# Keys of even and odd columns from one TensorE matmul, and a rotary product that writes to other partitions than it reads

## The chip, the core and the metric

The kernel runs on one core of one Trainium2 chip. The metric is device time in microseconds (us). Three runs of the kernel before gave 519.69, 520.85 and 522.8 us; the median, 520.85 us, is the time before.

## What is computed

Two layers on x of 8 sequences by 256 tokens by 128 columns. Each layer normalises x, and adds an attention and a mixture of experts of the normalised x. The change lies in the second layer's attention, which has 16 query heads and 4 key heads of 8 columns each, with a rotary position code on queries and keys:

```python
def _apply_rotary(x, freqs):
    x1, x2 = (x[..., ::2], x[..., 1::2])
    cos, sin = (jnp.cos(freqs), jnp.sin(freqs))
    return jnp.concatenate([x1 * cos - x2 * sin, x1 * sin - x2 * cos], axis=-1)
...
q = (x @ Wq + bq).reshape(Bx, Tx, NH, HD).transpose(0, 2, 1, 3)
k = (x @ Wk + bk).reshape(Bx, Tx, NKV, HD).transpose(0, 2, 1, 3)
q = _apply_rotary(q, freqs)
k = _apply_rotary(k, freqs)
scores = jnp.einsum('bhqd,bhkd->bhqk', q, k) / jnp.sqrt(jnp.float32(HD))
```

## The kernel before

The work goes by sequence (called a batch in the code, b = 0 to 7) and layer (L = 0, 1). A hand-written plan (`attention_plan`) is a list of items in steps t = 0 to 18. Each engine walks the same list and does its part of each item, in that order, waiting on semaphores. A step has 12 units u. In step t four batches are in flight: `a` is projected (`qk`, `hi`, `lo`, `stack`, `val`), `b` has its natural-order scores and their row maxima taken (`nat`, `max`), `c` its transposed scores and exponentials (`st`, `exp`), `d` its output finished (`pv`, `otr`, `norm`, `ott`, `proj`, `res`). The second layer's batches are projected in steps 8 to 15. Between steps 13 and 14 stands the second layer's mixture of experts (`moe`), with GpSimd's scatters (`scat`, from step 12) before it and its gathers (`back`) behind it.

The order at the head of a second-layer step is what the change touches. All of it is in unit 0, in this order:

- TensorE, `qk`: waits for PSUM banks M1 and M0 and multiplies the transposed x (256 columns) by WqA and WqB, the even and odd columns of Wq, into M1[:, 0:256] and M1[:, 256:512] (L1428), then by WkA and WkB into M0[0:32, 0:256] and M0[0:32, 256:512] (L1431). Then come `nat` and `st` of unit 0, the last `pv` of `d` (L1520), and unit 1.
- VectorE, `rotary` (L1079): waits for M1, writes (even + bias)*cos and (odd + bias)*sin of the queries to slots 0 and 1 of ROT; waits for M0, writes the same of the keys to slots 2 and 3 on partitions 0 to 31 (L1088), and raises `rot_ok`. A row maximum of `b` (L1059) follows.
- GpSimd, `rotate` (L726): waits for `rot_ok`, subtracts slot 1 from slot 0 and slot 3 from slot 2 (L731), raises `rsub_ok`.
- ScalarE, `high` (L802): waits for `rsub_ok`, copies the rounded values to XQ (L814, L815). Only behind that stands the first exponential (L824) of `c`, which frees a bank that `st` of unit 2 needs. There are two such banks, S0 and S1.
- In unit 1, VectorE's `low` (L1063) waits for ScalarE's copy and writes the rounding rest (L1075), ahead of the row maximum of unit 1.

The keys' weights lie side by side in WP[1][:, 512:...] as 32 even and 32 odd columns. The biases lie in a table of constants, one column for even and one for odd, on partitions 0 to 31. The tables cosr and sinr repeat every 8 partitions, so that any block of 32 partitions holds the same values.

Of the kernel before, what the change touches and what calls it, by code (L numbers as in the profile page):

```python
# [11 lines left out]
ALU = mybir.AluOpType  # L12
# [3 lines left out]
P = 128  # L16
NB, T, C = 8, 256, 128
NT = NB * T // P
TPB = T // P
NH, HD = 16, 8  # L20
NKV = 4
# [31 lines left out]
CO_BQ = CO_STEP + E1  # L53
# [8 lines left out]
def constants(w):  # L62

    t = np.zeros((P, NCONST), np.float32)
    r, c = np.arange(P)[:, None], np.arange(P)[None, :]
    t[:, CO_ID:CO_ID + P] = r == c
    t[:, CO_MASK:CO_MASK + P] = np.where(c > r, NEG, 0.0)
    t[:, CO_TRI:CO_TRI + P] = r < c
    t[:, CO_ONE:CO_ONE + P] = 1.0
    inv = (np.float32(1.0) / np.float32(10000.0) ** (np.arange(0, HD, 2, dtype=np.float32) / np.float32(HD))).astype(np.float32)  # L70
    ang = (np.arange(T, dtype=np.float32)[None, :] * inv[:, None]).astype(np.float32)
    cos, sin = np.cos(ang).astype(np.float32), np.sin(ang).astype(np.float32)
    for row in range(P):
        i = row % HD
        a, b = (cos, sin) if i < HD // 2 else (sin, cos)
        t[row, CO_C:CO_C + T] = a[i % (HD // 2)]
        t[row, CO_S:CO_S + T] = b[i % (HD // 2)]
    t[:, CO_I8:CO_I8 + E0] = np.arange(E0)
    t[:, CO_IN:CO_IN + CAP] = np.arange(1, CAP + 1)
    for r in range(4):  # L80
        t[QK_ROWS + 2 * r:QK_ROWS + 2 * r + 2, CO_SEL + r] = 1.0
    t[:, CO_THR:CO_THR + NT] = P * np.arange(NT)
    t[:, CO_PRE:CO_PRE + E1 * E1] = (np.arange(E1)[None, :] < np.arange(E1)[:, None]).reshape(-1)
    t[:, CO_J:CO_J + NTILE] = np.arange(NTILE)
    home = [expert_home(e) for e in range(E1)]
    t[:, CO_STEP:CO_STEP + E1] = np.append(np.diff(home), 0)
    t[:, CO_BQ], t[:, CO_BQ + 1] = w["L0_attn_bq"], w["L0_attn_bk"]
    for a in range(2):
        t[:, CO_BQ + 2 + a] = halves(w["L1_attn_bq"], a)
        t[0:NKV * HD, CO_BQ + 4 + a] = halves(w["L1_attn_bk"], a)  # L90
    t[:, CO_B1:CO_B1 + E0 * HC] = w["L0_ffn_b1"].reshape(E0 * HC, P).T
    t[:, CO_B2:CO_B2 + E0] = w["L0_ffn_b2"].T
    t[:, CO_RW:CO_RW + E1] = w["L1_ffn_router_w"].T
    t[:, CO_LN], t[:, CO_LN + 1] = w["L1_ffn_ln_scale"], w["L1_ffn_ln_bias"]
    for e in range(E1):
        t[:, CO_UB + home[e]:CO_UB + home[e] + HC] = w["L1_ffn_up_b"][e].reshape(HC, P).T
    return t


def halves(x, a):  # L100

    x = x.reshape(x.shape[:-1] + (-1, 1, HD // 2, 2))[..., a]
    return np.concatenate([x, x], axis=-2).reshape(x.shape[:-3] + (-1,))
# [10 lines left out]
def expert_home(e):  # L114

    return (e // 3) * (KS + 16) + KS + 4 + 4 * (e % 3)
# [185 lines left out]
def build(nc, w, table, wp_d, moe_d, out):  # L302
    ctx = ExitStack()
    with ctx:
        def sb(name, shape, dt=F32):
            return ctx.enter_context(nc.sbuf_tensor(name, shape, dt))

        def sem(name):
            return ctx.enter_context(nc.semaphore(name))
# [10 lines left out]
        cosr, sinr = K[:, CO_C:CO_C + T], K[:, CO_S:CO_S + T]  # L320
        identb, maskb, trib, oneb = (sb(n, [P, P], BF16) for n in ("identb", "maskb", "trib", "oneb"))
        WP = [sb(f"WP{L}", [P, x.shape[1]]) for L, x in enumerate(wp_d)]
# [2 lines left out]
        Wo = [WP[0][:, 3 * C:4 * C], WP[1][:, 2 * C + 96:3 * C + 96]]  # L325
        Wr = WP[0][:, 4 * C:4 * C + E0]
        WqAB = WP[1][:, 0:2 * C].rearrange("c (j n) -> c j n", j=2)
        WkAB = WP[1][:, 2 * C:2 * C + 64].rearrange("c (j n) -> c j n", j=2)
        bcol = K[:, CO_BQ:CO_BQ + 6]
        bvb = [sb(f"bvb{L}", [P, C]) for L in range(2)]  # L330
        bob = [sb(f"bob{L}", [P, C]) for L in range(2)]
# [18 lines left out]
        ROT = [sb(f"ROT{i}", [P, 4, T]) for i in range(2)]  # L350
# [56 lines left out]
        bank = {n: ctx.enter_context(nc.psum_tensor(f"ps_{n}", [P, 512], F32)) for n in names}  # L407
# [6 lines left out]
        full = {n: sem(f"full_{n}") for n in names}  # L414
# [106 lines left out]
        def await_free(eng, n, use):  # L521

            if before[n, use] is not None:
                eng.wait_ge(*released(before[n, use]))

        def await_full(eng, n, use):

            eng.wait_ge(*filled[n, use])
# [435 lines left out]
        def _(dve):  # L964
# [9 lines left out]
            for i in range(NV):  # L974
                last = dve.memset(VA[i][:], 0.0)
# [103 lines left out]
            def rotary(b):  # L1079

                i = b % 2
                if b >= 2:
                    dve.wait_ge(qlo_ok, NB + b - 1)
                dve.wait_ge(rc_ok, 1)
                for j, (n, rows, col) in enumerate((("M1", P, 2), ("M0", NKV * HD, 4))):
                    await_full(dve, n, ("qk", 1, b))
                    for a, tab in ((0, cosr), (1, sinr)):
                        last = dve.scalar_tensor_tensor(out=ROT[i][0:rows, 2 * j + a, :],  # L1088
                                                        in0=bank[n][0:rows, a * T:(a + 1) * T],
                                                        scalar=bcol[0:rows, col + a:col + a + 1], in1=tab[0:rows, :],  # L1090
                                                        op0=ALU.add, op1=ALU.mult)
                last.then_inc(rot_ok, 1)

            def values(L, b):
# [238 lines left out]
            def attention(plan):  # L1333
                for at, item in enumerate(plan):
# [5 lines left out]
                    if k == "qk" and item[1] == 1:  # L1340
                        rotary(item[2])
# [40 lines left out]
        def _(pe):  # L1382
            mm = pe.matmul
            M0, M1 = bank["M0"], bank["M1"]
# [31 lines left out]
            def qk(L, b):  # L1416
                x = XT[:, T * b:T * (b + 1)]
                if L == 0:
                    await_free(pe, "M1", ("qk", L, b))
                    for j in range(2):  # L1420
                        last = mm(M1[:, T * j:T * (j + 1)], Wqk0[:, j, :], x, start=True, stop=True)
                    last.then_inc(full["M1"], 1)
                else:
                    await_free(pe, "M1", ("qk", L, b))
                    await_free(pe, "M0", ("qk", L, b))
                    pe.wait_ge(f_in, 16 * 5)
                    for j in range(2):
                        last = mm(M1[:, T * j:T * (j + 1)], WqAB[:, j, :], x, start=True, stop=True)  # L1428
                    last.then_inc(full["M1"], 1)
                    for j in range(2):  # L1430
                        last = mm(M0[0:32, T * j:T * (j + 1)], WkAB[:, j, :], x, start=True, stop=True)  # L1431
                    last.then_inc(full["M0"], 1)

            def val(L, b):
                n = C if L == 0 else NKV * HD
# [264 lines left out]
            def ffn():  # L1700
# [4 lines left out]
                with pe.Fori(0, E0 - 1, 2) as e0:  # L1705
# [14 lines left out]

            layer1 = {"py": slots_out, "po": combine, "px": xt, "pl": logits}
            work = {"qk": qk, "val": val, "nat": nat, "st": st, "pv": pv, "mxt": mxt, "otr": otr, "ott": ott,
                    "proj": proj}

# [51 lines left out]
```

## Time and profile before

| | |
|---|---|
| median of the runs | 520.85 us (519.69 to 522.8) |
| time of the profiled execution | 522.24 us |
| its span in the profile | 520.2 us |
| mean granted TensorE clock in it | 0.96 of full speed |
| busy: TensorE, VectorE, ScalarE, GpSimd | 87%, 62%, 48%, 33% of the span |
| second-layer `qk` of batches 0 to 7 starts at | 212.2, 234.1, 255.3, 276.9, 297.6, 323.4, 438.3, 459.7 us |

The profiled execution is 1.4 us above the median; its span is 2.0 us under its own time. PE is TensorE's matmuls, PEld its weight loads, which run ahead of the matmuls; DVE is VectorE, ACT ScalarE, POOL GpSimd. One fp32 matmul of the program appears as two matmul records. Ends of matmuls are modelled. A granted clock of 1.00 is 2.4 GHz and 0.50 is 1.2 GHz. In brackets behind a row stands how long its engine had been idle before it, and what ended that.

### The profile page before, as it was taken

What the parts mean: (1) busy time and instruction counts of PE and PEld (TensorE: products, weight loads), DVE (VectorE), ACT (ScalarE), POOL (GpSimd) and SP (SyncE); (2) the same over time, 40 slices, a digit from 0 to 9 for tenths busy, and PEclk for the clock granted to TensorE, in tenths of its full rate; (3) what the DMA queues carried; (4) which work ended last, traced back from release to release, by engine and by line L of the source; (5) the groups of instructions that cost most, each with busy time, mean ns of one, the idle gap of its engine ahead of it and who ended that gap; (6) DMA issues with size and microseconds to landing.
All of it is one profiled execution on the core that took longest, in us unless ns stands there. A gap on an engine that the chain in (4) does not pass through costs nothing.

```text
span 520.2 us, 10264 instructions
## 1 busy us (share of the span) xinstructions
PE 452.7 (87%) x3503; PEld 343.1 (66%) x3503; DVE 322.6 (62%) x974; ACT 248.0 (48%) x564; POOL 173.7 (33%) x226
## 2 busy tenths in 40 slices
PE   1668899979999999999988987894999999898985
PEld 1554567758868878677665663663999997554643
DVE  5565741126668868777787795642666665565672
ACT  1731455524655655454464442442565563644452
POOL 6640120003254354444544417771000000737600
PEclk9998999997999999999999997896999999899898
DMA  5553123473223233021162612231221211314220
GB/s 163 134 129 89 63 64 107 122 211 114 68 74 99 69 90 115 15 79 42 42 202 95 192 59 70 87 97 56 62 81 44 81 58 36 102 43 135 52 58 28
DMA packets 51441, 45.89 MB, mean 88 GB/s; under 512 B 4968, under 2 KB 46464, under 8 KB 51392
## 3 DMA queue, kind: packets, MB, share of 16 engines
q1 hardware_dynamic: 47424, 35.54, 23.9%
q0 software_dynamic: 2240, 4.53, 3.2%
q10 hardware_dynamic: 1728, 5.20, 3.0%
q8 instruction: 27, 0.44, 0.3%
q14 instruction: 22, 0.18, 0.1%
HBM read 26.24 MB, written 19.01 MB: 87 GB/s over the span
## 4 chain that ended last, share of the span: by engine, by line
PE 49%; issue 23%; DVE 9%; POOL 8%; DMA 5%; ACT 3%; SPq 1%; ACTq 0%; DVEq 0%; POOLq 0%
PE ps_S L1498 7%; PE ps_P L1520 6%; POOL xs L742 6%; PE ps_N L1469 6%; PE ps_N L1465 4%; PE ps_M L1717 3%; PE ps_M L1563 2%; PE ps_M L1600 2%; PE ps_P L1537 2%; DMA X<-in_L_attn_x 2%; PE ps_P L1554 2%; DVE NM L1059 2%; PE ps_N L1710 2%; PE ps_S L1710 2%; PE ps_M L1574 1%
## 5 line engine op out<-in xcount | busy, mean ns | idle before, releaser
L824 ACT ACTIVATE PT<-ps_S 128x512 f32<-128x512 f32 x192 | 112.6, 592 | 98.5 <-PE ps_S L1498 96.6
L1059 DVE TENSOR_REDUCE NM<-ps_N 128x2 f32<-128x512 f32 (+1 forms) x192 | 128.0, 682 | 46.0 <-PE ps_N L1469 44.8
L1469 PE MATMUL ps_N<-STK 96*128 96x256 f32 (+1 forms) x256 | 103.2, 446 | 0.0
L689 POOL TENSOR_SCALAR_AFFINE_SELECT PT<-PT 128x512 f32<-128x512 f32 x80 | 49.1, 638 | 142.5 <-ACT PT L824 142.5
L1498 PE MATMUL ps_S<-STK 100*128 100x128 f32 (+5 forms) x352 | 92.8, 339 | 3.2 <-ACT PT L824 3.2
L1465 PE MATMUL ps_N<-maskb,identb 128*128 128x256 bf16 (+1 forms) x192 | 62.2, 324 | 6.7 <-DVE NM L1059 6.3
L1498 PEld LDWEIGHTS ps_S<-STK 104*128 104x128 f32 (+1 forms) x352 | 62.3, 199 | 7.5 <-ACT PT L824 4.5
L1520 PE MATMUL ps_P<-PT,VA 128*32 128x256 f32 (+1 forms) x1024 | 56.8, 341 | 0.4 <-ACT PT L824 0.4
L1469 PEld LDWEIGHTS ps_N<-STK 96*128 96x128 f32 x256 | 52.0, 203 | 4.7 <-issue 0.7
L731 POOL TENSOR_TENSOR ROT<-ROT 128x256 f32<-128x256 f32 (+1 forms) x16 | 11.3, 731 | 104.2 <-DVE ROT L1088 104.2
L1520 PEld LDWEIGHTS ps_P<-PT,VA 128*32 128x32 f32 x1024 | 27.2, 111 | 26.8 <-issue 12.6
L916 ACT ACTIVATE LATE<-ps_N,ucol 128x128 f32<-128x128 f32 x104 | 29.6, 369 | 19.3 <-PE ps_N L1666 18.1
L742 POOL DMA_INDIRECT xs<-XN,slot x32 | 31.1, 973 | 19.8 <-DVE slot L1254 10.5
L1465 PEld LDWEIGHTS ps_N<-maskb,identb 128*128 128x128 bf16 x192 | 20.0, 104 | 22.9 <-DVE NM L1059 10.9
L1495 PE MATMUL ps_S<-identb,maskb 128*128 128x256 bf16 (+1 forms) x72 | 24.0, 334 | 7.7 <-ACT PT L824 4.7
L1666 PE MATMUL ps_N<-LATE 128*128 128x128 f32 x208 | 29.6, 288 | 0.5 <-DVE LATE L1280 0.3
L1666 PEld LDWEIGHTS ps_N<-LATE 128*128 128x128 f32 x208 | 26.6, 200 | 1.6 <-issue 0.6
L1283 DVE COPY LATE<-EW 128x512 f32 x39 | 16.6, 427 | 13.7 <-PE ps_P L1676 7.8
L1329 DVE TENSOR_SCALAR LATE<-ps_M,consts 128x320 f32 x8 | 4.4, 551 | 33.2 <-PE ps_M L1717 33.2
L1275 DVE COPY LATE<-EW 128x512 f32 x39 | 16.8, 430 | 10.7 <-issue 5.2
L814 ACT ACTIVATE XQ<-ROT 128x256 fp32r<-128x256 f32 x8 | 3.3, 417 | 39.1 <-POOL ROT L731 39.1
L1676 PE MATMUL ps_P<-LATE 128*128 128x128 f32 x160 | 21.3, 276 | 0.3 <-ACT LATE L916 0.3
(197 smaller groups left out, 818.3 us busy)
## 6 DMA issues: line engine op xcount, KB each, us to landing
STK<-scr SPq DMA_DIRECT2D x96, 96.0 KB
scr<-XQ SPq DMA_DIRECT2D x24, 256.0 KB
ROT<-in_L_ffn_W SPq DMA_DIRECT2D x16, 256.0 KB, 3.1
EW<-in_moe ACTq DMA_DIRECT2D x8, 512.0 KB, 3.4
scr<-XQ SPq DMA_DIRECT2D x24, 128.0 KB
xs<-zero SPq DMA_DIRECT2D x1, 2496.0 KB, 11.1
LATE<-xs SPq DMA_DIRECT2D x9, 256.0 KB, 2.8
ysl<-LATE SPq DMA_DIRECT2D x9, 256.0 KB, 2.3
```

Source lines behind the costliest of these rows:

```text
L689: last = pool.affine_select(out=v, in_=v, compare_op=ALU.is_ge, fill=0.0, base=0, pattern=[[0, 4], [1, P]], channel_multiplier=-1)
L742: pool.indirect_dma_start(xs, bass.IndirectOffsetOnAxis(ap=slot[:, i, k:k + 1], axis=0), XN[:, i, :], None)\
L824: act.activation(PT[:, g, r, :], bank[s][:], ACT.Exp, scale=SCALE).then_inc(exp_ok, 1)
L916: act.activation(E_H[j % 2][:, P * m:P * (m + 1)], bank[UP_BANKS[j % 3]][:, P * m:P * (m + 1)], ACT.Gelu, bias=ucol[j % 2][:, m:m + 1]).th ...
L1059: dve.tensor_reduce(NM[b % 2][:, h, qt, :].rearrange("q (p c) -> q c p", p=2)[:, slots[0]:slots[-1] + 1, :], bank[s][:].rearrange("q (c p ...
L1465: mm(diag, identb[:], maskb[:, None, :].broadcast_to((P, many, P)), start=True, stop=False, skip_group_check=True)
L1469: last = mm(s[:, 2 * w_ * i:2 * w_ * (i + 1)], stk[0:QK_ROWS, c, P * qt:P * (qt + 1)], stk[0:QK_ROWS, k_slots(L, c, 2 * h, 2), 0:w_], star ...
L1495: mm(s[:].rearrange("k (h q) -> k h q", h=len(slots))[:, :, 0:P], maskb[:], identb[:, None, :].broadcast_to((P, len(slots), P)), start=Tru ...
L1498: last = mm(s[:, n * i:n * (i + m)], stk[rows, k_slots(L, c, g, 1), P * kt:P * (kt + 1)], stk[rows, c:c + m, T - n:T], start=not masked, s ...
L1520: last = mm(o, va[:, kt, head, :], pr, start=(kt == 0), stop=(kt == 1))
L1666: last = mm(o[:, P * m:P * (m + 1)], E_W1[j % 2][:, P * m:P * (m + 1)], E_XT[j % 2], start=True, stop=True)
L1676: last = mm(bank[DOWN_BANKS[j % 2]][:, 0:C], E_H[j % 2][:, P * m:P * (m + 1)], E_W2[j % 2][:, P * m:P * (m + 1)], start=(m == 0), stop=(m ...
```

## The change

One matmul per batch, with all 64 columns of the keys' weights, writes the even half to M0[0:32, 0:256] and the odd half to M0[32:64, 0:256]. The odd half's rotary product reads PSUM, bias and table on partitions 32 to 63 and writes ROT on partitions 0 to 31, as before. The bias of the odd half moves to partitions 32 to 63. The counts of semaphores and their places in the order stay as they are.

```diff
@@ constants
-        t[0:NKV * HD, CO_BQ + 4 + a] = halves(w["L1_attn_bk"], a)
+        t[NKV * HD * a:NKV * HD * (a + 1), CO_BQ + 4 + a] = halves(w["L1_attn_bk"], a)
@@ build
-        WkAB = WP[1][:, 2 * C:2 * C + 64].rearrange("c (j n) -> c j n", j=2)
+        WkAB = WP[1][:, 2 * C:2 * C + 64]
@@ rotary
-                for j, (n, rows, col) in enumerate((("M1", P, 2), ("M0", NKV * HD, 4))):
-                    await_full(dve, n, ("qk", 1, b))
-                    for a, tab in ((0, cosr), (1, sinr)):
-                        last = dve.scalar_tensor_tensor(out=ROT[i][0:rows, 2 * j + a, :],
-                                                        in0=bank[n][0:rows, a * T:(a + 1) * T],
-                                                        scalar=bcol[0:rows, col + a:col + a + 1], in1=tab[0:rows, :],
-                                                        op0=ALU.add, op1=ALU.mult)
+                tabs = (cosr, sinr)
+                await_full(dve, "M1", ("qk", 1, b))
+                for a in range(2):
+                    dve.scalar_tensor_tensor(out=ROT[i][:, a, :], in0=bank["M1"][:, a * T:(a + 1) * T], scalar=bcol[:, 2 + a:3 + a],
+                                             in1=tabs[a], op0=ALU.add, op1=ALU.mult)
+                await_full(dve, "M0", ("qk", 1, b))
+                for a in range(2):
+                    r = slice(NKV * HD * a, NKV * HD * (a + 1))
+                    last = dve.scalar_tensor_tensor(out=ROT[i][0:NKV * HD, 2 + a, :], in0=bank["M0"][r, 0:T],
+                                                    scalar=bcol[r, 4 + a:5 + a], in1=tabs[a][r, :], op0=ALU.add, op1=ALU.mult)
@@ qk
-                    for j in range(2):
-                        last = mm(M0[0:32, T * j:T * (j + 1)], WkAB[:, j, :], x, start=True, stop=True)
-                    last.then_inc(full["M0"], 1)
+                    mm(M0[0:64, 0:T], WkAB, x, start=True, stop=True).then_inc(full["M0"], 1)
```

## Rows read from the trace of the kernel before

**Rows 1.** Profile page: span, busy time, and the chain that ended last by engine

```profile
span 520.2 us, 10264 instructions
...
PE 452.7 (87%) x3503; PEld 343.1 (66%) x3503; DVE 322.6 (62%) x974; ACT 248.0 (48%) x564; POOL 173.7 (33%) x226
...
PE 49%; issue 23%; DVE 9%; POOL 8%; DMA 5%; ACT 3%; SPq 1%; ACTq 0%; DVEq 0%; POOLq 0%
```

**Rows 2.** Groups by line and shape: busy us, mean ns of one, idle before

```profile
L1431 PE MATMUL ps_M<-XT,WP 128*32 128x256 f32 x32 | 8.4, 385 | 0.0
L1088 DVE SCALAR_TENSOR_TENSOR ROT<-ps_M,consts 32x256 f32<-32x256 f32 x16 | 6.9, 467 | 0.1
```

**Rows 3.** Chain that ended last: start us, us, what; batches 0, 4 and 6

```profile
213.30 0.98 PE ps_M L1431 x4
...
217.10 0.40 ACT XQ L815
...
299.34 0.58 DVE ROT L1088 x2
...
453.46 0.68 PE ps_P L1554 x4
```

**Rows 4.** Waits over the whole span: us in total, times, longest

```profile
ACT XQ L814 <- POOL ROT L731: 39.1, 8, 5.6
```

**Rows 5.** Timeline of batch 0's projection: start us, us, engine, line

```profile
213.23 1.05 PE L1431 MATMUL ps_M<-XT,WP 128*32 128x256 f32 x4
213.41 1.77 DVE L1088 SCALAR_TENSOR_TENSOR ROT<-ps_M,consts 128x256 f32<-128x256 f32 x4 [0.18 <-PE ps_M L1428]
...
215.11 0.67 DVE L1059 TENSOR_REDUCE NM<-ps_N 128x4 f32<-128x512 f32 x1
215.26 1.42 POOL L731 TENSOR_TENSOR ROT<-ROT 128x256 f32<-128x256 f32 x2 [1.88 <-DVE ROT L1088]
...
216.77 0.42 ACT L814 ACTIVATE XQ<-ROT 128x256 fp32r<-128x256 f32 x1 [4.69 <-POOL ROT L731]
...
217.53 0.75 DVE L1075 TENSOR_TENSOR XQ<-ROT,XQ 128x256 fp32r<-128x256 f32 x2 [1.75 <-ACT XQ L815]
...
218.03 0.66 PE L1498 MATMUL ps_S<-STK 100*128 100x128 f32 x4 [0.80 <-ACT PT L824]
```

**Rows 6.** Timeline of VectorE in batch 1: the four rotary products one by one

```profile
235.37 0.48 DVE L1088 SCALAR_TENSOR_TENSOR ROT<-ps_M,consts 128x256 f32<-128x256 f32 x1 [0.45 <-PE ps_M L1428]
...
235.77 0.48 DVE L1088 SCALAR_TENSOR_TENSOR ROT<-ps_M,consts 128x256 f32<-128x256 f32 x1
...
236.28 0.47 DVE L1088 SCALAR_TENSOR_TENSOR ROT<-ps_M,consts 32x256 f32<-32x256 f32 x1
...
236.68 0.46 DVE L1088 SCALAR_TENSOR_TENSOR ROT<-ps_M,consts 32x256 f32<-32x256 f32 x1
```

**Rows 7.** Timeline of batches 4 to 7: TensorE's wait behind each projection

```profile
303.06 0.39 PE L1495 MATMUL ps_S<-identb,maskb 128*128 128x512 bf16 x1 [0.57 <-ACT PT L824]
...
327.44 1.43 POOL L731 TENSOR_TENSOR ROT<-ROT 128x256 f32<-128x256 f32 x2
...
330.22 0.39 PE L1495 MATMUL ps_S<-identb,maskb 128*128 128x512 bf16 x1 [1.54 <-ACT PT L824]
...
445.60 0.39 PE L1495 MATMUL ps_S<-identb,maskb 128*128 128x512 bf16 x1 [2.00 <-ACT PT L824]
...
465.53 0.39 PE L1495 MATMUL ps_S<-identb,maskb 128*128 128x512 bf16 x1 [0.55 <-ACT PT L824]
...
472.05 0.68 PE L1554 MATMUL ps_P<-WP,ONT 128*128 128x128 f32 x4
```

**Rows 8.** Busy time by stretch: PE, PEld, DVE, ACT, POOL, granted clock, DMA, GB/s

```profile
216.00:220.00 4.00, 3.20 (x26) 2.76 (x25) 2.47 (x6) 3.10 (x8) 0.94 (x2) 1.00 0.04 8
...
333.00:334.00 1.00, 1.00 (x7) 0.94 (x6) 0.55 (x2) 0.14 (x1) 0.84 (x1) 0.50 0.21 74
...
448.00:449.00 1.00, 1.00 (x6) 0.84 (x4) 0.69 (x4) 0.00 (x0) 0.93 (x1) 0.50 0.28 66
```

## The prediction

> **What bounds the kernel now.** I read the page first. TensorE is busy for 87% of the span and carries 49% of the chain that ended last [rows 1]. So an edit that takes matmuls away looks worth its full price, and the reader should distrust that: the share is an average, and what counts is whether TensorE is waited for just behind the matmul that goes. I looked for that in the chain, in the waits, and then in the timeline of each projection.
>
> In batch 0 the chain does pass through the key matmuls: 0.98 us for the two of them [rows 3]. But 3.8 us later it leaves TensorE and goes through ScalarE's copy of the rotated keys (217.10). The timeline shows why [rows 5]. Two paths leave the query matmul:
>
> - TensorE's own: key matmuls, then scores and `pv` of units 0 and 1, then a wait. The second-next `st` needs a bank that the first exponential frees, and TensorE sat idle 0.80 us until 218.03.
> - The rotary path: four products on VectorE (213.41, 1.77 us in all), GpSimd's subtractions (215.26, 1.42 us), ScalarE's copies (216.77), and only then the exponential.
>
> ScalarE was idle for 4.69 us before its copy, because `high` stands ahead of the exponentials in its order; over the eight batches this is 39.1 us, 5.6 us at most [rows 4]. VectorE is held at the same place: `low` waited 1.75 us for ScalarE's copy, with the next row maximum queued behind it [rows 5]. So the rotary path ends last, and TensorE has slack against it in every batch. The slack is 0.80 us in batch 0 [rows 5] and within 0.01 us of it in batches 1 to 3; it is 0.57, 1.54, 2.00 and 0.55 us in batches 4 to 7 [rows 7]. Not one of the eight is zero.
>
> **The change part by part.**
>
> *TensorE.* Half of the key matmuls goes. A matmul streams the same 256 columns of x whether 32 or 64 rows come out, so one of the two remains at its price: 0.98 / 2 = 0.49 us saved per batch [rows 3], and 8 x 0.49 = 3.9 us of TensorE's busy path in all (3503 matmul records become 3487 [rows 1]). The sum of recorded durations, 8.4 us for 32 records [rows 2], halves by 4.2, because records overlap. The weight load has 64 columns in place of two of 32, and runs ahead of matmuls in either case; I take nothing for it. What of the 3.9 us reaches the end? TensorE comes to its wait 0.49 us sooner and waits 0.49 us longer, since ScalarE is not ready sooner for it. The scores of unit 1 are ready sooner too, but their row maximum is queued behind `low`. Value: 0. If the slack were gone, the cost removed would show in full; that is the first rival.
>
> *VectorE, the wait for the keys.* In batch 1 the four products start at 235.37, 235.77, 236.28 and 236.68 [rows 6]. The first to the second, and the third to the fourth, are 0.40 us apart, although each takes 0.46 to 0.48 us: they overlap a little. The second to the third is 0.51 us. The third waits for M0, which is full 0.98 us behind M1. With the change M0 is full 0.49 us sooner, near 235.8, before the earliest possible start at 236.17. The wait goes: 0.51 - 0.40 = 0.11 us gained on the rotary path. A satisfied wait does not stop such an overlap: the row maximum behind the products started at 215.11 where they ended at 213.41 + 1.77 = 215.18 [rows 5].
>
> *VectorE, the moved product.* The fourth product reads partitions 32 to 63 and writes 0 to 31. No row of before shows a VectorE instruction that does so. The nearest row is the same product in place, 467 ns [rows 2], 0.40 us from start to start. Bound from below: it costs no less than now, as it has the same 256 elements on the same 32 partitions; a gain has no source. Bound from above for the likely case: it does not overlap its neighbour, 0.47 for 0.40 us, so 0.07 us lost. A much dearer one is a rival, below. So the rotary path gains 0.04 to 0.11 us per batch. I take 0.07, between ends this close.
>
> The Trainium skill speaks against this edit here: its page "VectorE: DVE Perf Modes", section "Two Vector instructions with no wait between them", says that an instruction whose operands or output start in another group of 32 partitions than those of the instructions before it starts only when all earlier ones have finished, and the one behind it likewise. By that rule the fourth product and the row maximum behind it would each lose the 0.07 us of overlap; the sum below would be about 520.6 in place of 520.4 us. The rows of before show the overlap, but nothing on other partitions.
>
> *GpSimd and ScalarE.* Same instructions on same tiles; nothing changes but the start.
>
> *Where the 0.07 us counts.* In batches 0 to 3, 6 and 7 TensorE waits for ScalarE behind the rotary path, so it counts in each. In batch 4 the chain runs through VectorE's products themselves, on to the routing [rows 3], so it counts too. In batch 5 GpSimd is busy with scatters and takes up its subtraction at 327.44 with no idle time before it [rows 7]; nothing. So 7 x 0.07 = 0.5 us.
>
> **Sum.** Against the profiled execution: 522.24 - 0.5 = 521.7 us, with a span near 519.7. Its own time is 1.4 us over the median, so against the median: 520.85 - 0.5 = 520.4 us. A measurement of this kernel can tell about 0.5% (2.6 us) from no change, and this is 0.1%.
>
> **The rivals.**
>
> *First, TensorE's 0.49 us comes back whole* (faster). For it: 87% busy, and the chain through L1431 in batch 0. Against it: eight waits of 0.55 us or more behind the spot. It would give 520.85 - 3.9 - 0.5 = 516.4 us. To reach 0.5% with the 0.5 us of the rotary path, some four or five of the eight batches must give their 0.49 us back. Chance 0.09.
>
> *Second, the longer wait brings the clock down* (slower). TensorE's wait in batches 0 to 3 grows from 0.80 to 0.80 + 0.49 - 0.07 = 1.22 us. Around batch 0's the granted clock was 1.00, 2.4 GHz [rows 8]. Behind the waits of 1.54 and 2.00 us in batches 5 and 6 [rows 7] it was 0.50, 1.2 GHz, at 333 and at 448 us [rows 8]. The new 1.22 lies between what was harmless and what was not, and the trace can't say on which side. The waits of batches 4 and 7 grow to 0.99 and 0.97; those of batches 5 and 6 have their fall already. Price: from TensorE's restart to the same matmul L1554 it is 453.46 - 445.60 = 7.86 us in batch 6 with the fall [rows 3, 7], and 472.05 - 465.53 = 6.52 us in batch 7 without it [rows 7], so 1.34 us a fall. With two falls 520.4 + 2.7 = 523.1, with three 524.4, with all four 525.8 us. It decides from the third: 3.1 us are needed, 2.3 falls. Chance that there are two or more: 0.22, of which 0.13 for three or four.
>
> *Third, the moved product is dear* (slower). If writing to other partitions took a second pass, the fourth product would cost 0.47 us more: 520.85 - 7 x 0.11 + 7 x 0.47 = 523.4 us. It decides from 0.48 us more per product. No row speaks for it or against it. Chance 0.04. The Trainium skill, "Vector Engine (DVE) Microarchitecture Reference", section on the reshape front-end, calls such moves of 32 partitions free; no run here shows it yet.
>
> *Fourth, the change doesn't do what it says*, if one matmul of 64 rows took as long as two of 32. Then the wait for M0 stays and 520.85 us comes out: no change as well. Chance 0.03, counted with the forecast's sign.
>
> **How the numbers follow.** No gain worth measuring: 0.62 for the forecast, whose own range with the scatter of the three runs is 519.0 to 522.3 us. Clock 0.22, TensorE's time back 0.09, dear product 0.04, no effect 0.03. The range for 8 in 10 leaves out the first rival's full sum and the clock's worst case, and takes in its two falls and part of the third: 518.3 to 524.2 us. Faster by over 0.5%: 0.10 (the first rival and a little scatter). Slower by over 0.5%: 0.18 (three or four falls 0.13, dear product 0.03, scatter 0.02). Same: 0.72.
>
> **What the profile of the changed kernel would show.** L1431's successor has 16 matmul records and 0.49 us a batch. The third product starts 0.40 us behind the second, the fourth 0.40 to 0.47 behind the third. ScalarE's wait for GpSimd is all but the same; TensorE's wait for the exponential is near 1.22 us in batches 0 to 3. The clock's row tells the second rival: if 0.50 stands anywhere between 215 and 300 us, it was right. The prediction is wrong if that is so, if TensorE's waits stay at 0.80 (the time came back), or if the moved product takes over 0.8 us.

## The result: slower, and slower than the range

Six runs of each kernel side by side gave a median of 526.71 us for the changed kernel (525.89 to 529.23) against 520.73 us (516.61 to 522.8) for the one before: a ratio of 1.0127, interval 1.0081 to 1.0173. The forecast was 520.4 us in a range up to 524.2. On two later occasions (below, 12 runs each) the same kernel came out at 1.0049 (1.0019 to 1.0079) and 1.0053 (1.0022 to 1.0084), so the sign is firm. The size was 1.3% once and 0.5% twice; the first interval and the second just miss each other, and what of this lies with the chip and what with the few runs is open. Medians in this document are of all executions; the ratios and intervals are worked out without those in a slower state, so a ratio is not the quotient of the medians beside it.

The page of the changed kernel, first lines and the chain by engine, against [rows 1]:

```profile
span 527.1 us, 10232 instructions
...
PE 458.4 (87%) x3487; PEld 348.6 (66%) x3487; DVE 323.6 (61%) x974; ACT 248.2 (47%) x564; POOL 173.3 (33%) x226
...
PE 46%; issue 23%; DVE 9%; POOL 9%; DMA 7%; ACT 4%; SPq 2%; ACTq 0%; DVEq 0%; POOLq 0%
```

TensorE has 16 matmul records fewer, as it should, and is busy 5.7 us longer. Fewer instructions, more busy time: the instructions themselves got slower. So the next view is the granted clock. A stage is the stretch from the start of one second-layer projection to the start of the next (batch 4's starts at 297.19 us in the kernel before, not at 297.6). Stages of batches 0 to 3, with time, busy time of PE, PEld, DVE, ACT, POOL, then the granted clock; first the kernel before:

```profile
212.17:234.13 21.96, 20.12 (x185) 15.66 (x181) 16.86 (x53) 10.96 (x24) 10.05 (x17) 1.00 0.16 49
234.13:255.27 21.14, 19.78 (x186) 15.63 (x182) 16.30 (x47) 10.84 (x24) 10.05 (x17) 1.00 0.17 52
255.27:276.89 21.62, 19.64 (x166) 13.30 (x162) 16.72 (x52) 10.85 (x24) 10.05 (x17) 1.00 0.46 147
276.89:297.19 20.30, 18.80 (x159) 12.64 (x155) 15.51 (x46) 9.86 (x22) 8.83 (x16) 1.00 0.51 156
```

The changed kernel, the same stages:

```profile
213.58:237.00 23.42, 21.22 (x184) 16.92 (x180) 17.23 (x53) 11.05 (x24) 10.02 (x17) 0.93 0.15 47
237.00:258.08 21.08, 19.35 (x183) 15.45 (x179) 16.36 (x47) 10.83 (x24) 10.01 (x17) 1.00 0.17 51
258.08:281.17 23.09, 20.80 (x163) 14.48 (x159) 17.08 (x52) 11.05 (x24) 10.02 (x17) 0.93 0.44 138
281.17:301.49 20.32, 18.41 (x158) 12.49 (x154) 15.61 (x46) 9.85 (x22) 8.82 (x16) 1.00 0.51 155
```

The stages of batches 1 and 3 are as before within 0.06 us. Those of batches 0 and 2 are longer by 1.46 and 1.47 us, and their mean clock is 0.93: the clock fell to half for a part of them. Such a fall is also called a dip below. The dip itself stands in narrower stretches of the changed kernel, same columns:

```profile
216.00:220.00 4.00, 2.84 (x32) 2.06 (x31) 2.35 (x6) 1.86 (x6) 1.40 (x2) 1.00 0.02 6
221.00:224.00 3.00, 3.00 (x16) 2.82 (x15) 2.61 (x9) 0.91 (x3) 1.22 (x2) 0.52 0.20 62
...
450.00:453.00 3.00, 2.94 (x11) 2.27 (x12) 1.55 (x3) 1.73 (x5) 2.38 (x3) 0.50 0.21 56
453.00:456.00 3.00, 3.00 (x15) 2.32 (x13) 1.91 (x7) 0.60 (x1) 2.35 (x3) 0.50 0.60 177
```

Up to 220 us the clock is 2.4 GHz, from 221 to 224 near 1.2 GHz. Behind batch 6 it stays at 1.2 GHz from 450 to 456 us. In the kernel before it was at 1.2 GHz at 448 us [rows 8] and back at 2.4 GHz by 451:

```profile
451.00:453.00 2.00, 2.00 (x16) 1.58 (x14) 1.17 (x2) 1.15 (x3) 1.47 (x2) 1.00 0.57 165
```

What stands ahead of the dip, in the timeline of batch 0's projection in the changed kernel, against [rows 5]:

```profile
214.64 0.65 PE L1433 MATMUL ps_M<-XT,WP 128*64 128x256 f32 x2
...
216.65 1.40 POOL L731 TENSOR_TENSOR ROT<-ROT 128x256 f32<-128x256 f32 x2 [1.86 <-DVE ROT L1093]
...
218.14 0.42 ACT L814 ACTIVATE XQ<-ROT 128x256 fp32r<-128x256 f32 x1 [4.65 <-POOL ROT L731]
...
219.39 0.66 PE L1499 MATMUL ps_S<-STK 100*128 100x128 f32 x4 [1.16 <-ACT PT L824]
```

TensorE's wait is 1.16 us in place of 0.80. In batch 1 it is 1.17, with no dip behind it.

The 6.9 us between the two spans (527.1 and 520.2) are made up as follows, from the starts of the projections in both. 1.4 us stands ahead of the first changed instruction (213.58 against 212.17), so it is put down to run-to-run scatter. Batches 0 to 3 give +1.46, -0.06, +1.47, +0.02; batch 4 -0.8; batch 5 with the experts behind it +1.0; batch 6 +1.4, where the dip is longer; batch 7 and the end +1.0. The two dips in batches 0 to 3 are thus 2.9 of the 6.9 us, and the longer one in batch 6 up to 1.4.

### The profile page after: what moved, and what is told of

Same layout as the page of the kernel before. It is cut to its first block, busy times and chain, and to the rows that moved or that the text cites. A ratio compares the mean times of both kernels' runs of the same rounds, so it can differ in the third digit from the quotient of the medians.

```text
span 527.1 us, 10232 instructions
## 1 busy us (share of the span) xinstructions
PE 458.4 (87%) x3487; PEld 348.6 (66%) x3487; DVE 323.6 (61%) x974; ACT 248.2 (47%) x564; POOL 173.3 (33%) x226
## 4 chain that ended last, share of the span: by engine, by line
PE 46%; issue 23%; DVE 9%; POOL 9%; DMA 7%; ACT 4%; SPq 2%; ACTq 0%; DVEq 0%; POOLq 0%
PE ps_S L1499 6%; POOL xs L742 6%; PE ps_N L1470 5%; PE ps_P L1521 5%; PE ps_N L1466 4%; PE ps_M L1718 3%; DMA scm<-MS 3%; PE ps_M L1564 2%; PE ps_M L1601 2%; PE ps_P L1538 2%; POOL ROT L731 2%; DMA X<-in_L_attn_x 2%; PE ps_N L1711 2%; PE ps_S L1711 2%; PE ps_P L1555 2%
## 5 line engine op out<-in xcount | busy, mean ns | idle before, releaser
L1470 PE MATMUL ps_N<-STK 96*128 96x256 f32 (+1 forms) x256 | 106.0, 458 | 0.0
L1499 PE MATMUL ps_S<-STK 100*128 100x128 f32 (+5 forms) x352 | 94.6, 345 | 5.1 <-ACT PT L824 4.8
L1466 PE MATMUL ps_N<-maskb,identb 128*128 128x256 bf16 (+1 forms) x192 | 63.9, 333 | 6.7 <-DVE NM L1059 5.8
L1470 PEld LDWEIGHTS ps_N<-STK 96*128 96x128 f32 x256 | 53.7, 210 | 5.1 <-issue 0.7
L742 POOL DMA_INDIRECT xs<-XN,slot x32 | 31.0, 970 | 19.8 <-DVE slot L1257 10.5
L1496 PEld LDWEIGHTS ps_S<-identb,maskb 128*128 128x128 bf16 x72 | 7.4, 102 | 22.3 <-ACT PT L824 10.5
```

What stands on the lines that cost most here:

```text
L742: pool.indirect_dma_start(xs, bass.IndirectOffsetOnAxis(ap=slot[:, i, k:k + 1], axis=0), XN[:, i, :], None)\
L1466: mm(diag, identb[:], maskb[:, None, :].broadcast_to((P, many, P)), start=True, stop=False, skip_group_check=True)
L1470: last = mm(s[:, 2 * w_ * i:2 * w_ * (i + 1)], stk[0:QK_ROWS, c, P * qt:P * (qt + 1)], stk[0:QK_ROWS, k_slots(L, c, 2 * h, 2), 0:w_], star ...
L1496: mm(s[:].rearrange("k (h q) -> k h q", h=len(slots))[:, :, 0:P], maskb[:], identb[:, None, :].broadcast_to((P, len(slots), P)), start=Tru ...
L1499: last = mm(s[:, n * i:n * (i + m)], stk[rows, k_slots(L, c, g, 1), P * kt:P * (kt + 1)], stk[rows, c:c + m, T - n:T], start=not masked, s ...
```

## The experiments

Two theories stood against each other. **Clock:** with half of the key work gone TensorE waits longer behind each projection, and behind some of these waits its clock falls. **Moved product:** the instruction on VectorE that writes to other partitions costs the time. The first four kernels happened to run on a chip on which the kernel before takes 566 us. In their profiles ScalarE's exponentials have 40.1 to 57.0 us of waits that the trace puts down to "remote", none of them before 300 us; in the profile of before they have none of that kind. What these waits are is not known. The ratios from there tell little. The stages of batches 0 to 3 come ahead of 300 us and can be read. So three of the four were run again elsewhere beside the changed kernel, and the fourth on a third occasion.

**The key matmul issued twice** (`e1_twice`, `r2_twice`). It gives TensorE its work back and leaves the moved product.

```diff
-                    mm(M0[0:64, 0:T], WkAB, x, start=True, stop=True).then_inc(full["M0"], 1)
+                    for _ in range(2):
+                        last = mm(M0[0:64, 0:T], WkAB, x, start=True, stop=True)
+                    last.then_inc(full["M0"], 1)
```

> The changed kernel with its key matmul of 64 rows issued twice into the same place, so that TensorE works as long in a projection as before the change; the moved rotary product stays. Clock theory (the change lengthens TensorE's wait behind each projection from 0.80 to about 1.2 us, and the clock falls to 1.2 GHz behind some of them): the waits go back to about 0.75 us, no fall between 215 and 300 us, and the time goes back to 520 to 521 us. Rival, the moved product is what costs: the time stays near 526.7 us. Rival, something in the placement of the program: no forecast.

565.48 us against 565.97, ratio 1.0008 (0.9980 to 1.0037).

> The key matmul of 64 rows issued twice, again. Clock theory: no fall in batches 0 to 3, 520 to 522 us where the kernel before takes 521. Moved product as the cause: as the changed kernel.

522.99 us against 522.15, ratio 1.0022 (0.9999 to 1.0044). The changed kernel in the same session:

> The changed kernel itself, once more beside the next three, since the first four runs came from a chip on which the kernel before takes 566 us. Clock theory: falls to 1.2 GHz behind one to three of the projections of batches 0 to 3, each lengthening its stage by about 1.5 us; on a chip where the kernel before takes 521 us, about 526.5 us.

524.91 us, ratio 1.0049 (1.0019 to 1.0079). The stages of batches 0 to 3 in the profile of the changed kernel of that session:

```profile
212.87:236.38 23.51, 21.31 (x184) 17.01 (x180) 17.24 (x53) 10.94 (x24) 10.02 (x17) 0.93 0.15 47
236.38:259.07 22.69, 20.96 (x184) 16.91 (x180) 16.66 (x47) 10.82 (x24) 10.04 (x17) 0.92 0.16 47
259.07:280.69 21.62, 19.25 (x163) 13.14 (x160) 16.81 (x52) 10.83 (x24) 10.02 (x17) 1.00 0.50 147
280.69:302.61 21.92, 20.01 (x158) 13.69 (x154) 15.99 (x46) 9.85 (x22) 8.81 (x16) 0.92 0.45 145
```

And with the matmul twice:

```profile
211.12:233.21 22.09, 20.15 (x186) 15.77 (x182) 17.06 (x53) 10.95 (x24) 10.04 (x17) 1.00 0.16 49
233.21:254.46 21.25, 19.80 (x186) 15.73 (x182) 16.46 (x47) 10.84 (x24) 10.04 (x17) 1.00 0.17 51
254.46:276.20 21.74, 19.67 (x165) 13.40 (x161) 16.89 (x52) 10.84 (x24) 10.03 (x17) 1.00 0.47 146
276.20:296.66 20.46, 18.85 (x160) 12.75 (x156) 15.71 (x46) 9.86 (x22) 8.82 (x16) 1.00 0.54 154
```

Three dips in the one, none in the other; four stages sum to 89.7 and 85.5 us. More work on TensorE made it 1.9 us faster in the median. The two intervals above are each against the kernel before and overlap; but the two kernels ran side by side, and the means of their 12 executions, 525.2 and 522.9 us, differ by 2.3 us with a 95% interval of 1.0 to 3.6 us (each execution taken as independent). The first session's profile of this kernel has no dip in batches 0 to 3 either. In the profile shown here the stages are each 0.11 to 0.16 us longer than in the kernel before, and TensorE's wait in batch 0 is 0.90 in place of 0.80 us:

```profile
217.10 0.66 PE L1501 MATMUL ps_S<-STK 100*128 100x128 f32 x4 [0.90 <-ACT PT L824]
```

From VectorE's first product to GpSimd's start it is 1.98 us here and 1.85 us in the kernel before. So about 0.1 us a batch is what the moved product costs when the wait for the keys stays.

**The product in place** (`e2_inplace`, `r3_inplace`): less work on TensorE, nothing on other partitions. The odd half of the keys is left out of the result; the instructions keep their number and shapes.

```diff
-                    r = slice(NKV * HD * a, NKV * HD * (a + 1))
+                    r = slice(0, NKV * HD)
```

> The changed kernel with one matmul of 64 rows, but the product for the odd half reads and writes partitions 0 to 31; the odd half of the keys is thereby left out of the result (it takes the even half with the odd half's table). Clock theory: slower than before, as the change, 525 to 527 us, with falls of the clock between 215 and 300 us. Rival, the moved product: back to about 520.7 us.

567.2 us against 565.97, ratio 1.0026 (0.9991 to 1.0061). Its stages of batches 0 to 3 took 23.3, 21.0, 23.0 and 20.2 us, with dips in the first and third: the same picture as the changed kernel's first profile.

```profile
211.93:235.25 23.32, 21.21 (x184) 16.95 (x180) 17.08 (x53) 10.96 (x24) 10.03 (x17) 0.93 0.16 47
...
256.23:279.22 22.99, 20.79 (x164) 14.47 (x160) 16.89 (x52) 10.99 (x24) 10.03 (x17) 0.93 0.44 138
```

> The changed kernel with the odd half's product in place on partitions 0 to 31 (the odd half of the keys is left out of the result). The first such run showed the falls in batches 0 and 2, a fourth product 0.40 us behind the third and TensorE's wait at 1.07 us. So: falls of the clock as in the changed kernel, time within 1 us of it (the moved product costs about 0.1 us a batch, 0.8 us in all), 0.2 to 1.0% over the kernel before. If the moved product were the main cost: within 0.2% of the kernel before.

524.51 us against 521.54, ratio 1.0027 (0.9991 to 1.0064). The profiled execution has one dip, in batch 3:

```profile
211.84:233.67 21.83, 19.72 (x183) 15.51 (x179) 16.78 (x53) 10.94 (x24) 10.02 (x17) 1.00 0.17 50
...
276.16:297.86 21.70, 19.97 (x158) 13.77 (x154) 15.81 (x46) 9.96 (x22) 8.80 (x16) 0.92 0.47 146
```

The changed kernel beside it:

> The changed kernel a third time, to be read beside the next three. Clock theory: one to three falls of the clock in batches 0 to 3, time 0.4 to 1.3% over the kernel before.

525.93 us, ratio 1.0053 (1.0022 to 1.0084), dips in batches 0, 1 and 3:

```profile
212.19:235.60 23.41, 21.21 (x184) 16.95 (x180) 17.23 (x53) 11.02 (x24) 10.02 (x17) 0.93 0.15 46
235.60:258.17 22.57, 20.84 (x183) 16.83 (x179) 16.65 (x47) 10.94 (x24) 10.02 (x17) 0.92 0.16 48
258.17:279.76 21.59, 19.22 (x163) 13.15 (x159) 16.78 (x51) 10.83 (x24) 10.02 (x17) 1.00 0.47 147
279.76:301.37 21.61, 19.79 (x157) 13.62 (x153) 15.82 (x46) 10.08 (x22) 8.81 (x16) 0.92 0.48 146
```

So dips come without the moved product. The in-place kernel's interval (0.9991 to 1.0064) holds no change as well as the changed kernel's ratio, so the times alone settle neither whether it is slower than the kernel before nor whether it is faster than the changed one. Its median is 1.4 us under the changed kernel's, where at most 1 us was expected. TensorE's wait behind batch 0 is 1.07 us in place:

```profile
217.56 0.66 PE L1499 MATMUL ps_S<-STK 100*128 100x128 f32 x4 [1.07 <-ACT PT L824]
```

**Filling the wait** (`e3_fill_after`, `r2_fill_after`): five bf16 matmuls into a bank whose next user overwrites them, in unit 2 of steps 8 to 15, ahead of that unit's natural-order scores, which are TensorE's last work before the wait. The two lines that the diff takes out never ran, as `WARM` is empty.

```diff
-                if u % 12 in WARM[L]:
-                    keep_clock(s)
+                if u == 2 and NB - 1 <= seq(L, b) < 2 * NB - 1:
+                    for _ in range(5):
+                        keep_clock(s)
```

> The changed kernel with five bf16 matmuls of 512 columns added in unit 2 of steps 8 to 15, just ahead of TensorE's wait for the first exponential (about 1.07 us of work at 2.4 GHz, whose result is overwritten). Clock theory: the wait is down to about 0.1 us in batches 0 to 3, near nothing in batches 4 and 7, and 1.3 us or more in batches 5 and 6; no fall behind batches 0 to 4, fewer behind 5 and 6: 517 to 521 us. Rival, that TensorE's work counts and not its clock: eight times up to 1.07 us more, so 527 us or above.

567.0 us against 565.97, ratio 1.0010 (0.9983 to 1.0037): neither theory's number, on that chip. Stages of batches 0 to 3: 21.9, 21.1, 21.6, 20.3 us, no dip.

> The changed kernel with five bf16 matmuls ahead of TensorE's wait, again. Clock theory: no fall in batches 0 to 3, so 4 us or more faster than the changed kernel, 519 to 522 us where the kernel before takes 521. If TensorE's amount of work counts: slower than the changed kernel.

519.74 us against 522.15, ratio 0.9962 (0.9937 to 0.9987): faster than before, and 5.2 us under the changed kernel beside it (the means differ by 5.4 us, 95% interval 3.9 to 6.9). Timeline of TensorE in batch 0; between the filling and the `st` there is no wait left to be named:

```profile
213.25 1.24 PE L1446 MATMUL ps_N<-maskb,identb 128*128 128x512 bf16 x5
...
214.92 0.66 PE L1500 MATMUL ps_S<-STK 100*128 100x128 f32 x4
```

Its stages of batches 0 to 3, and of batch 6:

```profile
209.11:231.03 21.92, 20.80 (x189) 15.99 (x185) 16.96 (x53) 10.94 (x24) 10.01 (x17) 1.00 0.17 50
231.03:252.11 21.08, 20.43 (x189) 15.95 (x185) 16.37 (x47) 10.83 (x24) 10.02 (x17) 1.00 0.17 51
252.11:273.71 21.60, 20.29 (x168) 13.63 (x165) 16.79 (x52) 10.83 (x24) 10.02 (x17) 1.00 0.48 147
273.71:294.02 20.31, 19.48 (x163) 12.97 (x159) 15.62 (x46) 9.85 (x22) 8.81 (x16) 1.00 0.49 156
...
435.24:455.02 19.78, 18.38 (x149) 11.48 (x149) 12.35 (x26) 10.36 (x20) 10.92 (x12) 1.00 0.35 96
```

The stage of batch 0 is 0.04 us shorter than in the kernel before: that is all that the change is worth there when the clock holds. Batch 6's takes 19.78 us, where the kernel before takes from 438.33 to 459.68, 21.35 us, with its dip.

**Filling the wait in the kernel before** (`e4_fill_before`, `r2_fill_before`): the same edit with four matmuls.

> The kernel before with four such matmuls in the same place (0.85 us of work). Clock theory: its wait of 0.80 us is filled in batches 0 to 3, and overfilled by 0.3 us in batches 4 and 7; the waits of batches 5 and 6 fall from 1.54 and 2.00 to 0.7 and 1.15 us and their falls of the clock go: 518 to 521 us. If only TensorE's work counts: 8 times 0.85, 527 us.

566.34 us against 565.97, ratio 0.9999 (0.9971 to 1.0027).

> The kernel before with four such matmuls, again. Batches 0 to 3 as before (no fall there to take away), any gain only from the falls behind batches 5 and 6: 518 to 521 us where the kernel before takes 521.

520.4 us against 522.15, ratio 0.9975 (0.9947 to 1.0003). Batches 0 to 3 as before (21.9, 21.1, 21.6, 20.3 us), batch 6 at 19.8 us. The interval just reaches no change.

**More filling where the waits are longest** (`r3_fill_more`, `r3_fill_before_more`): `range(5)` becomes 11 in the steps of batches 5 and 6 in the changed kernel, `range(4)` becomes 10 there in the kernel before.

> The changed kernel with five bf16 matmuls ahead of the wait, and eleven (2.35 us) in the steps of batches 5 and 6, whose waits are 2.75 and 2.37 us. Clock theory: no fall behind batches 0 to 7; the five alone gave 0.4% under the kernel before and still had waits of 2.06 and 1.31 us there without a fall, so this gains 0 to 1 us more: 518 to 520 us where the kernel before takes 522.

518.69 us against 521.54, ratio 0.9952 (0.9925 to 0.9979). It is faster than the kernel before, and its median is 7.2 us under that of the changed one in the same session. It is the lowest median here, but its ratio and that of the five alone (0.9952 and 0.9962) are not apart.

> The kernel before with four such matmuls, ten in the steps of batches 5 and 6. With the clock held in both, the change itself is worth about nothing: within 0.3% of the kernel before this one on the list.

520.89 us against 521.54, ratio 0.9972 (0.9938 to 1.0006). Its median is 2.2 us (0.42%) over the filled changed kernel's, where 0.3% were expected; the means of the two differ by 1.2 us with a 95% interval from -0.6 to 3.0, so no difference is shown. The profiles do differ in one place, in both sessions: batch 4's stage takes 24.96 us at a mean clock of 0.93 in the filled changed kernels, and 26.15 and 26.03 us at 0.87 in the filled kernels before. Why the clock is lower there for longer stays open.

## Why the prediction was wrong, point by point

*The step that failed* is the one in which the four lengthened waits were left with their clock. The prediction had the mechanism as its second rival, with the right place ("the new 1.22 lies between what was harmless and what was not"), and put only 0.22 on two or more falls, and no chance of its own on a single one. The profiles showed two falls in batches 0 to 3, then three, then three; the in-place kernel two and one. Together that is 11 falls behind 20 waits of 1.07 to 1.22 us. There is none behind the twelve waits of 0.80 to 0.92 us in batches 0 to 3 of the kernel before and of the one with the matmul twice (two profiles), none in batches 0 to 3 of the six profiles in which the wait was filled, and none behind the six of 0.94 to 0.99 us in batches 4 and 7 of the changed kernel. The likeliest case should have been two or three falls, for 523 to 524.5 us, and not none. How often the clock fell in the executions that were not profiled is not on record.

*The price of a fall* was put at 1.34 us, from batches 6 and 7. Over the eight falls in the three profiles of the changed kernel, each stage against the same one of the kernel before, it measured 1.31 to 1.62 us (1.46 and 1.47 in the first), so the price was nearly right. A fall lasts about 3.4 us, and half the clock over 3.4 us takes away 1.7 us of TensorE's work; nearly all of it shows in the stage.

*A term was missing:* the prediction said that batches 5 and 6 "have their fall already". A longer wait there made a longer fall: batch 6's stage went from 21.35 to 22.79 us in the first profile, with 1.2 GHz from 450 to 456 us. In the two later profiles of the changed kernel it was 21.3 and 21.4 us, so this comes in some runs only. It may be part of the difference between the first comparison and the later ones; no run tells.

*What TensorE saved.* Value 0 at the end: right. The stages without a dip in the three profiles of the changed kernel are the length they were, to 0.06 us, with 0.4 us less on TensorE. The size was put at 0.49 us a batch; from the start of the key matmuls to the next matmul it is 214.64 to 215.22, 0.58 us, against 213.23 to 214.21, 0.98 us, so 0.40. The wait came out at 1.16 us, for 1.22.

*The wait for the keys and the moved product.* VectorE's four products and the row maximum behind them, one by one, in the changed kernel (against [rows 6]):

```profile
214.82 0.48 DVE L1088 SCALAR_TENSOR_TENSOR ROT<-ps_M,consts 128x256 f32<-128x256 f32 x1 [0.18 <-PE ps_M L1431]
...
215.22 0.48 DVE L1088 SCALAR_TENSOR_TENSOR ROT<-ps_M,consts 128x256 f32<-128x256 f32 x1
215.61 0.46 DVE L1093 SCALAR_TENSOR_TENSOR ROT<-ps_M,consts 32x256 f32<-32x256 f32 x1
...
216.09 0.48 DVE L1093 SCALAR_TENSOR_TENSOR ROT<-ps_M,consts 32x256 f32<-32x256 f32 x1
...
216.59 0.69 DVE L1059 TENSOR_REDUCE NM<-ps_N 128x4 f32<-128x512 f32 x1
```

And in place (the kernel that keeps all products on their partitions, first session):

```profile
213.96 0.46 DVE L1093 SCALAR_TENSOR_TENSOR ROT<-ps_M,consts 32x256 f32<-32x256 f32 x1
...
214.36 0.46 DVE L1093 SCALAR_TENSOR_TENSOR ROT<-ps_M,consts 32x256 f32<-32x256 f32 x1
214.75 0.67 DVE L1059 TENSOR_REDUCE NM<-ps_N 128x4 f32<-128x512 f32 x1
```

The third product starts 0.39 us behind the second, as forecast: the wait for M0 is gone. The fourth starts 0.48 us behind the third in place of the 0.40 us that it is in the kernel in place and in [rows 6], the row maximum 0.50 behind the fourth in place of 0.39. Each instruction at the border of the other partitions waits for the one before it to end; the product itself takes 0.48 for 0.46 us. By the rule of the Trainium skill ("VectorE: DVE Perf Modes", "Two Vector instructions with no wait between them") both should lose their overlap, and the trace agrees, with 0.08 and 0.11 us lost. From the first product to GpSimd's start it is 1.85 us before [rows 5], 1.83 with the change and 1.73 in place. So the rotary path gained 0.02 us, not 0.07: the wait that went and the overlap that was lost cancel. The third rival (a second pass) did not come.

*Own range and chances.* With 0.10 for faster, 0.72 for same and 0.18 for slower, the case that came had 0.18. The top of the range, 524.2 us, is 0.64% over 520.85. The first comparison (1.27%) lies above it. The second and third (ratios 0.49% and 0.53%) lie inside it when each is taken against the kernel before of its own session, which took 522.15 and 521.54 us there; by the medians alone they are 0.5% and 0.8%. So by the ratios it is the first result alone that left the range, and why it was so much larger than the two later ones is not known.

**What stays open:** which of the waits of 1.1 to 1.2 us is followed by a fall. Batches 0 and 1 of the first profile have 1.16 and 1.17 us and only the first has one; in the two later profiles of the changed kernel both have one behind the same waits. Waits of 2.06 and 1.31 us in batches 5 and 6 of the filled changed kernel had none behind them; there the five dummy matmuls stand close ahead of the wait. The longer wait made falls more frequent, but its length alone doesn't decide. The runs don't separate the wait itself from the work missing ahead of it, either. And the first comparison's 6 us is more than its dips: the profile has 2.9 us from the two in batches 0 to 3 and up to 1.4 us from the longer one in batch 6.

## What to carry to other kernels

Where an engine's work is taken away ahead of a wait that something else ends, the gain is nil, and for TensorE the longer wait can cost: here 0.4 us of saved work a batch lengthened the wait, and each fall of the clock behind it took 1.3 to 1.6 us. Before such an edit, list the waits before and after, and mark those that come among or above the lengths that had a fall behind them; where neither row nor run decides, say so, and don't make "no fall" the likely case: here 11 of 20 such waits had one. Work that nobody needs, put into the wait, made the changed kernel 0.4 to 0.5% faster than the kernel before, and 1.0 to 1.4% faster in the median than itself without it, though its TensorE shows 87% busy. In the kernel before the same filling gave 0.25 to 0.28%, with intervals that just reach no change.

## What the runs showed of the hardware that was not expected

- The clock fell to 1.2 GHz behind 11 of 20 waits of 1.07 to 1.22 us, in stages where TensorE is 90% busy (21.22 of 23.42 us, the fall included), each time for about 3.4 us. Behind a wait of 2.37 us in batch 6 it stayed down for over 6 us in one profile (450 to 456 us), and for about 3.4 us behind 2.38 us in another (`r2_after`, from 451.6 to 454.9 us).
- With dummy matmuls in the wait the clock held, and they cost nothing: five took 1.07 us in batch 0 (213.25 to 214.32 in `r2_fill_after`), whose stage took 21.92 us against 21.96 in the kernel before, and batch 6's stage took 19.78 us against 21.35.
- A VectorE product that writes to another block of 32 partitions takes 0.48 us against 0.46, and does not overlap the instruction ahead of it nor the one behind it, which costs 0.08 and 0.11 us.
